# Second attention: the bias goes into the neighbours' rows by a row of ones on TensorE, and ScalarE copies them out

## What is computed

```python
x = x + _L0_gnn_ref(_layernorm(x), adj, ...)      # attention 0
x = x + _L0_ffn_ref(_layernorm(x), ...)           # 8 experts with a capacity
x = x + _L1_gnn_ref(_layernorm(x), adj, ...)      # attention 1: the change is here
x = x + _L1_ffn_ref(_layernorm(x), ..., edge_index)   # edge attention, 4 experts, top 2

def _L1_gnn_ref(x, mask, W, a, bias):
    hidden = jnp.einsum('bni,oi->bno', x, W)
    av = jnp.einsum('bno,ko->bnk', hidden, a)
    attn1, attn2 = (av[..., 0], av[..., 1])
    attn = attn1[:, :, None] + attn2[:, None, :]
    attn = jax.nn.leaky_relu(attn, negative_slope=ALPHA)
    attn = jnp.where(mask > 0, attn, attn + NEG_INF)
    attn = jax.nn.softmax(attn, axis=-1)
    out = jnp.einsum('bnm,bmo->bno', attn, hidden) + bias
    return out
```

## Time and profile before

| what | value |
|---|---|
| median of three runs | 3344.37 us (3342.35 to 3344.78) |
| profiled execution, its own time | 3343.19 us |
| its span | 3341.2 us |
| busy: TensorE matmul, weight load | 1858.5 us (56%), 1296.2 us (39%) |
| busy: VectorE, ScalarE, GpSimd | 2124.8 us (64%), 1172.3 us (35%), 1828.0 us (55%) |
| second attention, first L263 to last L295 | 1469.5 to 1709.7 us |
| last search | 1809.3 us |

### The profile page before, as it was taken

One profiled execution on the slowest core, in us unless ns is written; L12 is line 12 of the kernel. 1 busy time (PEld: TensorE's weight loads), 2 busy tenths in 40 slices (PEclk: granted clock), 3 DMA queues, 4 the chain that ended last, 5 costly groups with the idle time before them and its releaser, 6 DMA issues. The chain is left out here.

```text
span 3341.2 us, 32288 instructions
## 1 busy us (share of the span) xinstructions
PE 1858.5 (56%) x9050; PEld 1296.2 (39%) x9105; DVE 2124.8 (64%) x4468; ACT 1172.3 (35%) x2425; POOL 1828.0 (55%) x1783
## 2 busy tenths in 40 slices
PE   0788756012678787338982354445554445554456
PEld 0677655011455555237872132222332222322223
DVE  7899977967898899876753244444444444444445
ACT  0666644232344343126861122222222222222222
POOL 4200000775344343227776777777777777777772
PEclk9988855555899998669975677777777677777777
DMA  6892000010111110221111121122221222221221
GB/s 234 289 393 78 0 13 0 31 33 31 32 35 50 39 55 21 79 80 27 31 36 41 31 45 35 38 45 43 45 44 33 42 45 43 45 42 35 42 43 39
DMA packets 172759, 197.44 MB, mean 59 GB/s; under 512 B 60217, under 2 KB 127072, under 8 KB 172032
## 3 DMA queue, kind: packets, MB, share of 16 engines
q1 hardware_dynamic: 107184, 118.69, 10.7%
q0 software_dynamic: 60160, 67.73, 9.9%
q10 hardware_dynamic: 5328, 9.97, 0.8%
HBM read 96.94 MB, written 105.25 MB: 61 GB/s over the span
## 5 line engine op out<-in xcount | busy, mean ns | idle before, releaser
L1370 POOL DMA_INDIRECT edge_rows<-node_table,edge_ids x1024 | 998.1, 975 | 313.2 <-issue 284.0
L1246 DVE TENSOR_TENSOR win_score<-win,masked 128x384 f32<-128x384 f32 x32 | 18.1, 564 | 693.8 <-DMA win<-edge_table,win_ids 692.6
L1492 PE MATMUL x_b_featT<-ident,x_feat 128*128 128x128 f32 x128 | 34.8, 427 | 690.9 <-PEq L1110 459.1
L1013 POOL DMA_INDIRECT token_results<-arena,token_of x160 | 205.2, 1283 | 342.1 <-ACT arena L954 295.0
L1026 POOL DMA_INDIRECT adjacent<-keys,row_ids x256 | 247.0, 965 | 191.1 <-issue 79.8
L518 DVE TENSOR_TENSOR sort_ping<-sort_pong 128x1024 f32<-128x1024 f32 (+1 forms) x240 | 292.5, 1259 | 71.9 <-ACT sort_pong L905 67.4
L1498 PE MATMUL x_b_hid<-x_featT,x_w 128*128 128x512 f32 x512 | 315.9, 773 | 28.1 <-PEq L1110 28.1
L98 ACT ACTIVATE arena<-x,shift,rstd 128x128 f32<-128x128 f32 (+1 forms) x640 | 262.4, 484 | 157.2 <-DMA slots<-arena,send 141.0
L518 DVE TENSOR_TENSOR sort_pong<-sort_ping 128x1024 f32<-128x1024 f32 (+1 forms) x240 | 292.6, 1260 | 30.8 <-ACT sort_ping L905 25.7
L1492 PEld LDWEIGHTS x_b_featT<-ident,x_feat 128*128 128x128 f32 x128 | 22.9, 217 | 696.2 <-issue 696.2
L1505 PEld LDWEIGHTS x_b_res<-x_w,x_hid 128*128 128x128 f32 x2048 | 252.8, 201 | 97.5 <-issue 97.5
(11 more groups left out here) (332 smaller groups left out, 4200.9 us busy)
## 6 DMA issues: line engine op xcount, KB each, us to landing
edge_table<-zeros SPq DMA_DIRECT2D x8, 5120.0 KB, 36.0
edge_rows<-node_table,edge_ids POOLq DMA_INDIRECT x1024, 2.4
arena<-slots SPq DMA_DIRECT2D x40, 260.0 KB, 2.6
slots<-zeros SPq DMA_DIRECT2D x2, 5120.0 KB
edge_table<-edge_rows SPq DMA_DIRECT2D x64, 160.0 KB, 1.8
out_dram<-x_y ACTq DMA_DIRECT2D x33, 256.0 KB, 2.0
adjacent<-in_adj_dram SPq DMA_DIRECT2D x32, 256.0 KB, 2.8
arena<-token_results SPq DMA_DIRECT2D x32, 256.0 KB, 2.8
```

What stands on the lines that cost most here:

```text
L1013: pool.indirect_dma_start(rows_dram, bass.IndirectOffsetOnAxis(token_of[:, n % 4, r:r + 1], 0), res[:, n % 2, r, :], None, bounds_check=TO ...
L1370: pool.indirect_dma_start(rows[:, u, c, :], None, table_dram, bass.IndirectOffsetOnAxis(ids[:, u, c:c + 1], 0)).then_inc(rows_in[u], 16)
```

## The change

In the second attention TensorE writes the bias to the bank of the neighbours' rows by a matmul of one partition (a row of 128 ones as weights, the bias as the moving row, 512 columns by a broadcast over the four graphs), and the four L263 matmuls accumulate onto it. ScalarE copies the bank out, behind its exponentials in the same turn. VectorE's addition (L295) is gone. Nothing else moves; the bias is still loaded to all partitions, and one of them is read.

```diff
@@ act_step, behind the exponentials @@
+            if live(a) and not self.first:
+                act.wait_ge(self.righted, a + 1)
+                ge(act, self.out_s, a - 3)
+                act.activation(self.right[:, a % 4, :, 0, :], self.b_right[:, :, 0, :], ACT.Copy).then_inc(self.right_s, 1)
@@ pe_step, the neighbours' rows of a @@
                 ge(pe, self.right_s, a)
+                if not self.first:
+                    pe.matmul(self.b_right[:, :, 0, :], w["row"], w["bias"].unsqueeze(1).to_broadcast([1, PER, FEAT]), start=True, stop=False)
                 for v in range(PER):
-                    last = pe.matmul(self.b_right[:, v, :, :], f[:, v, :], w["other"], start=True, stop=True)
+                    last = pe.matmul(self.b_right[:, v, :, :], f[:, v, :], w["other"], start=self.first, stop=self.first or v == PER - 1)
                 last.then_inc(self.righted, 1)
@@ dve_biased is removed, and its call in the loop @@
-        dve.wait_ge(self.righted, a + 1)
-        ge(dve, self.out_s, a - 3)
-        dve.tensor_tensor(self.right[:, a % 4, :, 0, :], self.b_right[:, :, 0, :],
-                          self.w["bias"].unsqueeze(1).to_broadcast([P, PER, FEAT]), ALU.add).then_inc(self.right_s, 1)
@@ weights of att1 @@
-                          "bias": W["bias1"][:, :], "other": W["other1"][:, :], ...
+                          "bias": W["bias1"][0:1, :], "row": ones[0:1, :], "other": W["other1"][:, :], ...
```

More of the change, by code:

```diff
@@ L288, in dve_scores @@
         dve.tensor_reduce(self.below[:, b % 2, :], self.score[:, b % 2, :, :], AX_X, ALU.max, negate=True).then_inc(self.below_s, 1)
-    def dve_biased(self, dve, a):
-        if not live(a):
-            return
-        dve.wait_ge(self.righted, a + 1)
-        ge(dve, self.out_s, a - 3)
-        dve.tensor_tensor(self.right[:, a % 4, :, 0, :], self.b_right[:, :, 0, :],
-                          self.w["bias"].unsqueeze(1).to_broadcast([P, PER, FEAT]), ALU.add).then_inc(self.right_s, 1)
     def dve_updated(self, dve, m):
@@ L398, in front @@
                          {"key_side": W["key_row1"][:, :], "query_side": W["query_row1"][:, :],
-                          "bias": W["bias1"][:, :], "other": W["other1"][:, :], "fill": fills[:, 1, :], "ones": ones[:, 0:1]},
+                          "bias": W["bias1"][0:1, :], "row": ones[0:1, :], "other": W["other1"][:, :], "fill": fills[:, 1, :], "ones": ones[:, 0:1]},
                          view, att_small, banks, masked_s, key_made)
@@ L740, in _ @@
                 att1.dve_scores(dve, n + 2)
-                att1.dve_biased(dve, n + 3)
                 att1.dve_updated(dve, n - 1)
```

## The result

After: 3385.78 us (median of 4, 3384.15 to 3392.72). Before, beside it on the same chip: 3343.36 us (3338.85 to 3344.78). The ratio is **1.0134, 95% interval 1.0122 to 1.0147**: 42 us slower, where 12.6 were forecast (3357.0). The profiled execution of after took 3384.15 us, its span is 3382.2.

A forecast was written before the change was run, and what follows sets the result against it. GpSimd's fetches wait for VectorE's searches, so the attention's and table's turns were taken to set the end. Lengthened turns gave +12.2 us at search 23, hence a median of 3356.6, plus 0.4 for half clock: 3357.0, range 3346 to 3364.

The forecast's parts named there:

- L295 off VectorE buys: From turn 12 of the second attention, removing L295 gains only 0.14 us a turn, as L354 then waits for L349.
- the row's price at full clock: Bias matmul on TensorE ahead of the table matmuls: 1.24 us a turn, bounds 0.86 and 2.4 (half clock).
- turn with a search, without: Second attention's turns with table work: 8.52 us with a search (7.42 before), 8.12 without (6.88 before).
- search 0: First comparison of gathered keys on VectorE, which releases GpSimd's fetch 2: 1.6 us later, bounds 0 and 3.
- search 8: Comparison of gathered keys on VectorE, 11.5 us behind the start of its gathers: at 1571.3.
- search 9: Comparison of gathered keys in turn 12, the first turn with table work: at 1586.7 against 1589.03 before.
- searches 9 to 21: Turns with attention and table work: 12 of 8.52, 4 of 8.12, plus 3.4 for norms, 138.1 us (121.53 before).
- searches 21 to 23: Next stretch of key comparisons: 13.7 us against 15.72 before, as the 1.43 us wait for keys goes.
- search 23: Comparison of gathered keys in turn 30: at 1738.5 against 1726.28, +12.2 us, carried unchanged to the end.
- Cold clock: Rival: idle gaps in turns 2 to 11 halve TensorE's clock, the row costs 2.4 there; +17 us, 3362; chance 0.14.
- Row cheap: Rival: the row costs 0.86 us, turns 8.14 and 7.74; about +5 us, 3349.5; chance 0.14.
- GpSimd paces: Rival: turns stay under 7.7 us, so GpSimd's fetches set the pace to the end; -1 us, 3343; chance 0.11.

The follow-up runs named there:

- copy only: The changed kernel without the row matmul: ScalarE copies the neighbours' rows out, the bias is left out; 0.9987 of the kernel before in its last run.
- the fourth group: Last set of runs, on one undisturbed chip against the kernel before (3342.15 us): copy only, full rows, the change again (1.0126), early searches.
- full rows: The changed kernel with the bias matmul over all 128 partitions, weights of 1/128, same place and two passes; 1.0027 of the kernel before in its last run.
- the row in bf16: The changed kernel with bias and ones rounded to bf16, one pass in place of two; 1.0023 of the kernel before.
- early searches: The kernel before with one search ahead of the second attention's loop and one in each of turns -2 and -1; 0.9925, earlier 0.9966, of the kernel before.

## Why the prediction was wrong

The direction and the path were right; one term of the sum was far too small. By the prediction's own steps:

| step | forecast | measured |
|---|---|---|
| L295 off VectorE buys | 0.14 us a turn | 7.30 for 7.42 in copy only: 0.12 |
| the row's price at full clock | 1.24 us | 1.24 |
| ScalarE's copy | 0 | copy only 0.9987: 0 |
| turn with a search, without | 8.52, 8.12 | 8.47, 8.12 at full clock |
| search 0 | 1.6 later | 3.1 later |
| search 8 | 1571.3 | 1574.78 |
| search 9 | 1586.7 | 1596.04 |
| searches 9 to 21 | 138.1 | 154.7 |
| searches 21 to 23 | 13.7 (15.72 before) | 15.68 |
| search 23 | +12.2 | +40.15 |

**The step that failed** is "searches 9 to 21: 138.1", because it costed every turn at full clock, on the strength of 0.98 in the dense stretch before. That clock was taken as a property of the stretch, and it is one of the work in it. The 16.6 us that are missing go with the half clock, 37 us of the stretch in place of 3.4; the fourth group gives 15.5 for it by another way. The repeat of the change in the fourth group has the same seven falls and 154.73 us. The upper bound of the row's price, 2.4 at half clock, was written down and then used only for the start, and the rival *Cold clock* put half clock only into turns 2 to 11, behind idle gaps, on the strength of one L263 at 2.07 at the start of the attention. That the row itself could bring it, in the fullest stretch, was no rival.

Search 9 came 9.3 us later than forecast, 3.5 of them up to search 8 and 5.9 behind it. A part of that is the *Cold clock* rival: the change ran at half clock from 1571.3 to 1581.6, 10.2 us in a row (before: 6.8), behind a stretch with TensorE busy 4.33 of 7.00 us. From search 8 to search 9 its mean clock was 0.84, which is 6.8 us at half speed and explains at most 3.4 of the 5.9; the rest is not split. In the repeat of the fourth group search 9 came at 1593.41, so some 3 us of this part differ from one execution to the next. That the fetches would cover the early turns failed too:

```profile
1574.78:1596.04 21.26, 21.26 (x122) 16.15 (x122) 8.38 (x25) 14.56 (x37) 12.95 (x14) 0.84 0.09 24
```

TensorE was busy in all of these 21.26 us of after, where the forecast had it done early and waiting.

The 2 us to be won back between searches 21 and 23 did not come. The wait of 1.43 for the keys did go, but ahead of search 23 L352 waits 5.42 us for L347 (before 3.94), and L347 runs at half clock there:

```profile
1764.48 1.74 PE L347 MATMUL banks<-gat_w,arena 128*128 128x24 f32 x8
```

It was 1.74 in before too, so the clock had fallen in this turn already there (4.8 us of searches 21 to 23 at half speed, and 7.3 in the change). VectorE waited as long as before, 5.42 for 3.94 and 1.43: the wait for the keys was no slack.

Added up from the forecast of +12.2 at search 23: 9.3 more at search 9, 16.6 in the dense stretch and 2.0 behind it make 40.1, and 40.15 were measured.

Of the rivals, *Row cheap* (0.86, +5 us) has its own test in full rows: turns of 8.1 and 7.7 as worked out, but +9.3 in place of +5 by the medians, since the start and searches 21 to 23 gave nothing back (search 0 at 1499.40, search 9 at 1591.76, searches 21 to 23 15.58). *GpSimd paces* said a turn must stay under 7.7 us; the row in bf16, with 7.8, is the nearest, and it is 0.23% slower. The Trainium skill, page "TensorE: Matmul & The Clock Gate", section "Why this matters for your kernels", says that a single matmul over 32 rows takes the same time as over 128. No run here agrees for this fp32 matmul of 512 columns: with one partition or 32 it is 1.05 us to the next line, with 128 it is 0.86. The same section warns of idle gaps between bursts of matmuls as what costs the clock; that fits the fall of before (5.39 of 7.00 busy) and two of the seven in the change (5.23 and 5.28), and not the five behind the rows (6.74 of 7.00).

## What to carry to other kernels

When work moves onto an engine, ask not only how long it takes but what it does to the speed of what follows it: here a matmul over one partition, in a stretch that TensorE paces, cost its own 1.24 us a turn and then, through the clock, 15.5 us more over 16 turns. If a bias must go through TensorE, spread it over the partitions (1.0027 here) or make it one short pass (1.0023); and first see whether the engine that is relieved is the one waited for, since here the addition on VectorE was cheaper than every matmul that was tried. What did pay was found in the longest wait of the engine that paces the end, GpSimd's 28.95 us ahead of fetch 2.

## What the runs showed that I had not expected

- With a two-pass row over one partition of 128 the granted clock fell from 2.4 to 1.2 GHz while TensorE had next to no idle time (6.74 of 7.00 us busy): five times in 155 us with one row a turn. With two rows a turn there were eleven falls in the 191 us between searches 9 and 21, all of them inside the rows. With 32 partitions there were three, with 128 one and in bf16 two, and these, but for one of the 32 partitions', came behind stretches in which TensorE had idled. The runs show that the falls go with the row's few partitions and its two fp32 passes; by what measure of the work the clock is set they do not show.
- One and 32 partitions cost alike at full clock (1.05 us from the row to the next line); 128 cost less (0.86).
- On two of the four chips of the experiments every version took some 16% longer, with long waits for which the profile names no releaser (97.0 us in 13 of them in copy only). The change's loss was 0.9% there instead of 1.3%, and the gain of early searches 0.3% instead of 0.75%; full rows and copy only changed places between the two.
